# A third unit's scores before the last down product, softmax V three units behind, weight buffers renumbered

## What is computed

```python
xn = _layernorm(x)
s = attn(xn)     # pressure = q k^T * scale; causal mask to -10000;
                 # attn = 1 - tanh((pressure - threshold) / tau)**2, rows divided by their sum
h = rmsnorm(xn, norm1_w); scores = q k^T * scale; attn = softmax(scores)
X = xn + ctx @ wo
h2 = rmsnorm(X, norm2_w)
shared = (silu(h2 @ sh_gate) * (h2 @ sh_up)) @ sh_down
eout = (silu(gate) * up) @ e_down        # for each of 8 experts, weighed by a top-2 router
x = x + s * silu(X + shared + spec)
```

## Time and profile before

| | |
|---|---|
| three runs | 1149.21 us median, 1147.17 to 1158.49 |
| profiled execution | 1157.05 us, of which the span of the trace is 1155.2 us |
| PE busy | 1032.3 us, 89% |
| DVE busy | 856.3 us, 74% |
| ACT busy | 652.9 us, 57% |
| POOL busy | 347.4 us, 30% |
| chain that ended last | PE 56%, DVE 21%, ACT 11%, DMA 4%, issue 3% |

### The profile page before, as it was taken

The page is one execution under the profiler, slowest core; times in us unless marked ns, Lnnn a source line. Parts: engine busy times, 40 slices in busy tenths (PEclk is TensorE's granted clock), DMA queues, the critical chain, the costliest instruction groups (busy, mean ns, idle before and its releaser), DMA issues.

```text
span 1155.2 us, 18598 instructions
## 1 busy us (share of the span) xinstructions
PE 1032.3 (89%) x6912; PEld 471.8 (41%) x6912; DVE 856.3 (74%) x1716; ACT 652.9 (57%) x888; POOL 347.4 (30%) x194
## 2 busy tenths in 40 slices
PE   3459999989999999999999899999999889999998
PEld 1102355324652346423554245522465235542364
DVE  7447687759977597786877589775986869774872
ACT  4027862588326972378624884269723786248831
POOL 6500335103630154303352035400552033520023
PEclk9558999999999999999999999999999999999999
DMA  5540225103441045201251024310342113500020
GB/s 176 117 54 2 49 68 132 34 2 77 109 68 29 3 96 127 38 20 44 64 141 25 11 63 122 69 28 2 96 116 41 30 29 69 148 9 20 1 75 9
DMA packets 71785, 69.65 MB, mean 60 GB/s; under 512 B 8528, under 2 KB 63056, under 8 KB 71568
## 3 DMA queue, kind: packets, MB, share of 16 engines
q1 hardware_dynamic: 68928, 64.41, 24.7%
q10 hardware_dynamic: 2768, 4.06, 1.0%
HBM read 53.37 MB, written 14.81 MB: 59 GB/s over the span
## 4 chain that ended last, share of the span: by engine, by line
PE 56%; DVE 21%; ACT 11%; DMA 4%; issue 3%; SPq 3%; POOL 1%; ACTq 0%; DVEq 0%; POOLq 0%
PE O L1019 9%; PE O L1035 8%; DVE nmax L677 7%; DVE PT L714 7%; ACT PT L554 6%; PE S L1051 6%; PE S L1053 5%; PE S L994 5%; PE S L1052 5%; PE M L963 4%; PE M L960 4%; PE M L946 2%; DVE PT L840 2%; SPq L337 2%; SPq L327 1%
## 5 line engine op out<-in xcount | busy, mean ns | idle before, releaser
L554 ACT ACTIVATE PT<-S 128x1024 f32<-128x1024 f32 (+1 forms) x448 | 420.7, 971 | 117.3 <-PE S L994 115.0
L677 DVE TENSOR_REDUCE nmax<-M 128x1 f32<-128x512 f32 x512 | 330.6, 685 | 119.4 <-PE M L960 80.4
L714 DVE SCALAR_TENSOR_TENSOR PT<-PT 128x768 f32<-128x768 f32 (+1 forms) x192 | 215.6, 1171 | 96.4 <-ACT PT L554 96.0
L1019 PE MATMUL O<-PT,V 128*12 128x256 f32 (+3 forms) x2816 | 242.2, 424 | 0.0
L423 POOL TENSOR_TENSOR split<-split,parts 128x512 f32<-128x512 f32 x32 | 91.0, 2844 | 433.2 <-ACT parts L514 433.2
L438 POOL TENSOR_TENSOR PT<-PT,CB 128x1024 f32<-128x1024 f32 x56 | 133.2, 2385 | 278.0 <-DMA CB<-scrC 158.2
L588 ACT ACTIVATE PT<-S 128x1024 f32<-128x1024 f32 x72 | 73.9, 1027 | 250.7 <-PE S L1053 250.6
L994 PE MATMUL S<-stackQ,stackK 64*128 64x512 bf16 (+3 forms) x1024 | 192.1, 347 | 21.6 <-DMA stackQ<-mTZ 8.4
L1051 PE MATMUL S<-h2hi,wgu_hi 128*128 128x512 f32 x288 | 150.5, 522 | 0.1
L1035 PE MATMUL O<-PT,wdn 128*128 128x512 f32 x288 | 142.7, 595 | 0.0
L960 PE MATMUL M<-KX,stackQ 128*128 128x512 bf16 x256 | 104.3, 409 | 28.5 <-DMA KX<-scrK 21.3
(11 more groups left out here) (189 smaller groups left out, 1042.5 us busy)
## 6 DMA issues: line engine op xcount, KB each, us to landing
CB<-scrC SPq DMA_DIRECT2D x64, 256.0 KB, 5.7
stackQ<-scrQ SPq DMA_DIRECT2D x192, 64.0 KB
stackK<-scrK SPq DMA_DIRECT2D x192, 64.0 KB
scrQ<-parts SPq DMA_DIRECT2D x16, 384.0 KB, 5.0
scrK<-parts SPq DMA_DIRECT2D x16, 384.0 KB, 7.8
KX<-scrK SPq DMA_DIRECT2D x96, 32.0 KB
PT<-in_w_gu ACTq DMA_DIRECT2D x2, 1152.0 KB, 8.0
xin<-in_x SPq DMA_DIRECT2D x8, 256.0 KB, 2.9
```

The lines of the kernel that those rows point to most:

```text
L554: a.activation(PT[:, n % SLOTS, 2 * q * w:2 * q * w + 2 * w].rearrange("p (r n) -> p r n", r=2), S[k][:, :].rearrange("p (r n) -> p r n", ...
L677: v.tensor_reduce(nmax[:, h % 2, h // 2, t:t + 1], M[k][:, :], AX.X, ALU.max, negate=True).then_inc(m_read[k], 1)
L714: v.scalar_tensor_tensor(p, p, 1.0, p, ALU.subtract, ALU.mult).then_inc(weighed, 1)
L1019: last = t_.matmul(O[k][32 * q:32 * q + VW, i0:i1], V[:, j, 4 * g + q, :], PT[:, n % SLOTS, w * q + at:w * q + at + i1 - i0], start=(j == ...
```

## The change

Four things are changed together.

1. TensorE computes the scores of three units of the next row, not two, before the last down product: `SEAM = 3`. Unit 0's stand where they stood, unit 1's too, and unit 2's come behind the `x1` products.
2. In the rest of stage 1, V's product stands three units behind the scores, as in stage 2. In unit 3 it stands behind everything else. Units 14 and 15 of it stand whole in unit 17.
3. The slots of `PT` are renumbered, `slot(n) = (n + 3) % 4`: unit 0 takes slot 3, which no expert uses; unit 1 slot 0, unit 2 slot 1, unit 3 slot 2.
4. Y's maxima stand otherwise: two in unit 0, two in unit 1 (both before the last down product now), none in unit 2, six each in units 3 and 4. Z's stand four to a unit. `out_by_s`, the tanh (`gate`) and `out_gated` follow behind units 2 and 3.

```diff
+SEAM = 3
+def slot(n):
+    return (n + SLOTS - 1) % SLOTS
-spread(MAX["Y"], {0: 1, 1: 3, 2: 4, 3: 4, 4: 4})
-spread(MAX["Z"], {5: 3, 6: 4, 7: 4, 8: 5})
-PLACES[3].insert(2, "outT")
+spread(MAX["Y"], {0: 2, 1: 2, 3: 6, 4: 6})
+spread(MAX["Z"], {5: 4, 6: 4, 7: 4, 8: 4})
+PLACES[4].insert(3, "outT")
...
-                done = {0: 0, 1: 1, 2: DEPTH}
+                done = {1: 0, 2: 1, 3: DEPTH}
...
-                for n in range(2, UNITS):
+                for n in range(SEAM, UNITS):
                     names = u.places[n]
                     weights(it, n, 0)
+                    if n == SEAM and it > 0:
+                        gate(it - 1)
...
-                    if n == 0 and it > 0:
+                    if n == SEAM - 1 and it > 0:
                         out_by_s(it - 1)
-                    if n == 1 and it > 0:
+                    if n == SEAM and it > 0:
                         out_gated(it - 1)
...
-                v_at = {n: n - 2 for n in range(2, N1 + 2)} | {n: n - 3 for n in range(N1 + 3, UNITS)}
+                v_at = {n: n - 3 for n in range(SEAM, UNITS) if n not in (N1 + 1, N1 + 2)}
...
+                        elif n == N1 + 1:
+                            with_v(it, N1 - 2 + i // 2)
                         elif v_at.get(n, N1) < N1 and v_at[n] % NT > 0:
                             with_v(it, v_at[n], i // 2)
-                        elif n in v_at and i == 1:
+                        elif n in v_at and i == (3 if n == SEAM else 1):
                             with_v(it, v_at[n])
...
                 last.then_inc(down_done, 1)
+                if following:
+                    third_scores(ROWS[it + 1], it + 1)
                 for _step in second_product(it, NE - 1):
                     pass
```

More of the change, by code:

```diff
@@ L553, in weights, with gate @@
                 act.wait_ge(s_full[k], c + 1)
-                a.activation(PT[:, n % SLOTS, 2 * q * w:2 * q * w + 2 * w].rearrange("p (r n) -> p r n", r=2),
+                a.activation(PT[:, slot(n), 2 * q * w:2 * q * w + 2 * w].rearrange("p (r n) -> p r n", r=2),
                              S[k][:, :].rearrange("p (r n) -> p r n", r=2)[:, :, 0:w],
                              ACT.Exp if n < N1 else ACT.Sigmoid).then_inc(s_read[k], 1)
+            def gate(it):
+                act.wait_ge(out_scaled, it + 1)
+                a.activation(gT[:, :], O[0][:, :], ACT.Tanh, scale=0.5).then_inc(o_read[0], 1)
             def row(u, it, following):
                 bt = it + 1
-                outs = {**{NT * G + NT + (2 if G < NG - 1 else 1): G for G in range(NG)}, **{N1 + 3 * g + 6: NG + g for g in range(NG - 2)},
+                outs = {**{NT * G + NT + (3 if G < NG - 1 else 1): G for G in range(NG)}, **{N1 + 3 * g + 6: NG + g for g in range(NG - 2)},
                         UNITS - 1: 2 * NG - 2}
-                for n in range(2, UNITS):
+                for n in range(SEAM, UNITS):
                     names = u.places[n]
                     weights(it, n, 0)
+                    if n == SEAM and it > 0:
+                        gate(it - 1)
                     for name in names[:len(names) // 2]:
@@ L586, in row @@
                     if e < DEPTH:
-                        act.wait_ge(pv_done, it * UNITS + UNITS + e + 1)
+                        act.wait_ge(pv_done, it * UNITS + UNITS + e + 2)
                     a.activation(AB[e % DEPTH], S[k][:, :], ACT.Silu).then_inc(s_read[k], 1)
@@ L597, in row @@
                     a.activation(warm[:, :], n1s[:, :], ACT.Exp)
[L598 to L604, removed]
+                    for n in range(SEAM):
+                        for q in range(2):
+                            weights(it + 1, n, q)
+                        if n == 0:
+                            take(u, "maxT_W", bt)
+                else:
+                    gate(it)
             tau()
@@ L620, in _ @@
                             a.activation(wgu_hi[:, :, i * F:i * F + F], gu_raw[i], ACT.Copy).then_inc(gu_hi, 1)
-            for n in range(2):
+            for n in range(SEAM):
                 for q in range(2):
@@ L712, in weigh @@
                 w = width(n)
-                p = PT[:, n % SLOTS, 2 * q * w:2 * q * w + 2 * w]
+                p = PT[:, slot(n), 2 * q * w:2 * q * w + 2 * w]
                 v.scalar_tensor_tensor(p, p, 1.0, p, ALU.subtract, ALU.mult).then_inc(weighed, 1)
@@ L1019, in with_v @@
                         last = t_.matmul(O[k][32 * q:32 * q + VW, i0:i1], V[:, j, 4 * g + q, :],
-                                         PT[:, n % SLOTS, w * q + at:w * q + at + i1 - i0],
+                                         PT[:, slot(n), w * q + at:w * q + at + i1 - i0],
                                          start=(j == 0), stop=(NT - 1 in js and j == js[-1] and half != 0))
@@ L1147, in first_scores, with second_scores, third_scores, row @@
                     scores(it, 0, q)
-            def row(u, it, following):
-                v_at = {n: n - 2 for n in range(2, N1 + 2)} | {n: n - 3 for n in range(N1 + 3, UNITS)}
+            def second_scores(u, it):
+                for q in range(2):
+                    scores(it, 1, q)
+                for name in u.places[0]:
+                    work(u, it, name)
+            def third_scores(u, it):
+                scores(it, 2, 0)
                 for name in u.places[1]:
                     work(u, it, name)
-                for n in range(2, UNITS):
+                scores(it, 2, 1)
+            def row(u, it, following):
+                v_at = {n: n - 3 for n in range(SEAM, UNITS) if n not in (N1 + 1, N1 + 2)}
+                for n in range(SEAM, UNITS):
                     if n == N1 - 1:
@@ L1187, in row @@
                     work(u, it, "maxT_W")
[L1188 to L1191, removed]
+                    second_scores(ROWS[it + 1], it + 1)
                 for t in range(NT):
@@ L1207, in _ @@
             first_scores(0)
[L1208 to L1211, removed]
+            second_scores(ROWS[0], 0)
+            third_scores(ROWS[0], 0)
             for it in range(B):
```

## The result

The changed kernel is slower. Its median over 20 runs is 1168.99 us (1150.61 to 1180.82), that of before over 20 runs 1155.7 us (1147.17 to 1160.34). The ratio is 1.0066, with a 95% interval of 1.0036 to 1.0096. It is taken without the runs of a kernel that lie more than 1.5% above its fastest, of which the changed kernel has 11; over all runs the two medians stand 1.15% apart. A second measurement on another occasion gave 1.0085, 1.0051 to 1.0119. The forecast was 1147.6 us, within 1139 to 1157, counted from the 1149.21 us that three runs of before had given.

A forecast was written before the change was run, and what follows sets the result against it. TensorE was fullest at 89%, with VectorE pacing it up to unit 9 and ScalarE full behind. Terms of -0.6 and +0.4 gave -0.2 us a row, -1.6 over eight, so 1147.6 us, range 1139 to 1157.

The forecast's parts named there:

- Last down product: At the seam between rows: unit 2's scores ahead of it make it end 0.99 us later, some 0.3 waiting for ScalarE.
- Units 3 and 4: VectorE sets the pace with 12 of Y's maxima left instead of 15; unit 5's scores come 0.8 us earlier.
- Units 5 to 8: With 12 of Z's maxima instead of 13 in units 6 to 8, unit 9 comes 0.6 us earlier than before.
- Units 9 to 12: Part of units 9 to 17, where ScalarE is full and passes on the -0.6 us gained by unit 9.
- Unit 17: The V product still owed falls due here, whole products replacing halves; ScalarE, and VectorE behind it, lose 0.4 us.
- Sum of a row: -0.6 us by unit 9 and +0.4 in unit 17 give -0.2 us a row; distances hold from unit 18 on.
- The bounds of the seam: Per row -2.6 to +1.4 us, from a never idle VectorE to 0.99 lost unrecovered; -21 to +11 us overall.
- six maxima in a unit hold the scores back: Rival: units 4 and 5's scores stand behind maxima waiting for VectorE; 1156 or 1160 us; chance 0.13 for slower.
- sign that the whole is wrong: In the changed trace, unit 18 earlier or later by 1.4 us or more would make the whole prediction wrong.
- The base: The forecast's 1.6 us gain was taken off 1149.21 us, the median of the kernel before.
- Row 0: The first row, with no seam before it, was counted like the others, at -0.2 us.
- The sentence on slots: Renumbered slots and V three units behind cost and give nothing; the cover is one unit of TensorE's work.

The follow-up runs named there:

- e8: Changed kernel with unit 3's second and unit 4's two score pairs issued twice, and the late V product made up in unit 11: 1147.56 us, ratio 0.9953 to before.
- e3: Kernel before with only the new spread of Y's and Z's maxima, V still two units behind: 1156.93 us, ratio 1.0024 to before.
- e7: Changed kernel with three score pairs issued twice in each row, unit 3's second and unit 4's two: 1153.21 us, ratio 0.9983 to before.
- e9: Changed kernel with unit 3's second and unit 4's two score pairs issued twice in row 0 alone: 1161.89 us, ratio 1.0088 to before.
- e4: Kernel before with only V's products moved, to three units behind the scores in all of stage 1: 1174.92 us, ratio 1.0188 to before.

## Why the prediction was wrong, point by point

**The steps that held.** In rows at full clock the reckoning came out nearly as written, by the trace of after:

- *Last down product.* Predicted 0.99 us later behind unit 0's scores, measured 1.09 (5.44 us, 211.30 to 216.74, against 4.35). The 0.10 more is the change of tiles that was left out of the sum "since the pair waits for ScalarE at this place anyway". The pair started when reckoned, 5.12 us behind unit 0's scores, but held TensorE 0.32 us (216.42 to 216.74) and not 0.22: the wait for ScalarE lies ahead of the pair, and the change of tiles behind it.
- *Units 3 and 4.* Predicted -0.8 us at unit 5, measured -0.79. The order of events on VectorE is the one reckoned, down to its 0.58 us idle behind V's first product.
- *Units 5 to 8.* Predicted -0.6 us at unit 9, measured -0.53 (28.48 us behind the row's first exponential, against 29.01).
- *Units 9 to 12.* ScalarE was to pass the gain on. But unit 11's first weights stand 1.17 us earlier than before (32.27 against 33.44), since no V product was made up yet, and unit 12's only 0.54 (34.90 against 35.44). There TensorE waits 1.19 us for the DMA of Z's maxima, a wait that the prediction doesn't name, and it lets through about what the maxima had gained.
- *Unit 17.* Predicted +0.4 us, measured +0.48. e8 shows that it is the late V product: with that made up elsewhere, the 0.48 is gone. PE in the changed kernel, in unit 17 and at the start of 18:

```profile
257.17 0.28 PE L1001 MATMUL S<-never,identb 128*128 128x128 bf16 x2 [0.50 <-ACT PT L560]
...
258.64 0.28 PE L1001 MATMUL S<-never,identb 128*128 128x128 bf16 x2
...
261.06 0.38 PE L1001 MATMUL S<-never,identb 128*128 128x256 bf16 x2
```

- *Sum of a row.* Predicted -0.2 us, and the two rows without a fall are 0.16 and 0.26 shorter. That this fits so well is partly luck. At unit 18, where the -0.2 was to be seen (49.6 us behind unit 0's scores), it stood at 49.76 against 49.83 before, so only 0.07 was won, 0.05 by the weights. The rest came behind unit 18, where the prediction has every distance kept, and a good part of it among the experts, where the rows of before differ from each other by as much (135.03, 135.13, 135.47).

**The step that failed** is the frame of the sum: each duration was taken from rows at full clock, and the clock was not asked about anywhere. The text even says that TensorE waits more for VectorE in units 3 and 4 and that a V product is owed there, and prices only the time at which that product comes due, in unit 17. What that thinning does to the clock has no term, no bound and no rival: it was put at nothing without a reason. The runs showed in its place that the clock fell to half behind the seam, for 6.8 or 13.7 us in five of seven rows, and that this is the whole loss within the noise: with the clock kept up by three copied pairs of scores, the ratio went from 1.0085 to 0.9983. The bounds of the seam, -21 to +11 us, were bounds of waits alone. The rival on the other side, "six maxima in a unit hold the scores back", named the wrong mechanism, though its times, 1156 and 1160 us, lie on the right side; e3 shows that the six maxima alone cost 0.24%. The prediction's own sign that the whole is wrong, unit 18 later by 1.4 us or more, came in the five rows with a fall.

**The sizes.** By unit 18, row 3 had lost 2.2 us with 6.8 us at half clock, and row 4 had lost 4.2 us with 13.7 us at half (52.69 and 54.73 us, against 50.50 in a row without a fall). That is about a third of the time at half clock. A likely reason, which no run tests, is that in these units TensorE waits for VectorE and ScalarE a part of the time anyway. For each row -0.2 us was forecast. In five of the seven behind a seam stood +1.7 to +4.9 us instead.

**The base.** Forecast and result lie 21.4 us apart. Of these, 6.5 are in the time of before: 1149.21 us was the median of three runs, and twenty give 1155.7. The other 14.9 are the 13.3 us of loss and the 1.6 of gain that was forecast.

**Row 0** was counted like the others, "the same two tables". It runs at half clock at first, and the rise came 26.4 us behind its first exponential in place of 14.5. In e7, with copies, it came at 10.9 and the row lasted 133.8 us; in e9, with copies in row 0 alone, at 12.2 and 134.2.

**The sentence on slots**, "These edits cost and give nothing", said among others of V three behind, is the one that e4 contradicts most plainly. That edit alone costs 1.9%, of which unit 17, priced apart, is some 0.3.

The Trainium skill, "TensorE: Matmul & The Clock Gate", section "A second HAM failure mode: psum-queue depth-cycling", tells of a kernel in which frequent short idle times between groups of matmuls, and not one long one, made the clock go down and up again. The traces here agree: no wait of PE for VectorE at the changed seam is over 0.85 us in any row, and in five rows the clock fell there and rose again. It was not weighed before the run, and it speaks against this change.

**What stays open.** Why the falls come in rows 3 to 7 of one profile, in rows 3 and 4 of another and, by its clock, in hardly any row of the fastest run (1150.61 us, clock 0.971, no profile) isn't settled. Up to unit 4's first weights, all seven rows behind a seam run alike to 0.01 us, so what differs is not in the kernel's own work up to there; more than that the traces don't show. A kernel with the third scores alone, the maxima and V's products placed as before, was not run.

## What to carry to other kernels

When an edit moves matmuls out of a stretch in which TensorE already waits often, look at the granted clock there before adding up waits. A stretch that was dense only thanks to the moved work can fall to half clock, as in e4, and then costs more than the waits that were to be removed. Filling the stretch with matmuls whose result is not needed, ahead of a wait, is a cheap test of it, and can be a remedy (12.6 us here). Work moved away comes due somewhere: put it where TensorE waits for something else, as the DMA of Z's maxima in unit 11, and not where another engine waits for TensorE.

## What the runs showed of the hardware that was not expected

- The granted clock can fall to half behind short waits alone. In e4, waits of 1.06, 0.21 and 0.77 us stand at the first seam, with 2.42 us of work in the 4 us from 218 to 222, and the clock is 0.66 over the next 4.
- The same stretch is followed by a fall or not. In the changed kernel PE was busy 4.46 us of 6 in row 1, without a fall, and 4.45 in row 3, with one. Its runs spread over 30 us (1150.61 to 1180.82), the longer ones at the lower clocks, where those of before spread over 13.
- Redundant matmuls made a kernel faster: 0.6 us more of them in each row, and 12.6 us less in the median.
